# A two-layer token tower on one core: weight sums, head scales, spare products and low parts moved in the first attention

## The reference

```python
def act_quant(x):                       # one scale for the last axis
    scale = 127.0 / clip(max(abs(x), -1), 1e-5)
    return clip(round(x * scale), -128, 127) / scale
def bit_linear(x, W):                   # weights become -s, 0, +s
    s = clip(mean(abs(W)), 1e-5)
    return x @ (clip(round(W / s), -1, 1) * s).T
xq = act_quant(x)                       # x: the normalised tokens, 16 heads of 32
q, k, v = (act_quant(heads(bit_linear(xq, W))) for W in (Wq, Wk, Wv))
w = act_quant(softmax(q @ k.T / sqrt(32)))
y = act_quant(w @ v)                    # 4 positions of a sample attend to each other
x = x + act_quant(bit_linear(y, Wp))
# then: scores = x @ router_w, two of 16 experts; silu(x @ gate) * (x @ up) @ down
```

## Time and profile before

| | us |
| --- | --- |
| median of 3 runs | 303.21 |
| lowest, highest | 302.82, 305.16 |
| the profiled execution | 305.13 |
| its span, first to last instruction | 303.3 |
| TensorE, VectorE, ScalarE, GpSimd busy | 277.0, 237.1, 145.0, 14.4 |
| mean granted TensorE clock | 0.977 |

### The profile page before, as it was taken

One profiled execution on the slowest core, in us unless ns is written; L12 is line 12 of the kernel. 1 busy time (PEld: TensorE's weight loads), 2 busy tenths in 40 slices (PEclk: granted clock), 3 DMA queues, 4 the chain that ended last, 5 costly groups with the idle time before them and its releaser, 6 DMA issues. The chain is left out here.

```text
span 303.3 us, 4708 instructions
## 1 busy us (share of the span) xinstructions
PE 277.0 (91%) x1814; PEld 239.3 (79%) x1814; DVE 237.1 (78%) x438; ACT 145.0 (48%) x236; POOL 14.4 (5%) x32
## 2 busy tenths in 40 slices
PE   8988279959989999999999999987899999999993
PEld 3743144959988899999999988866799999999862
DVE  1789998593876999899989896698627896787683
ACT  2879550102844556556555423332128783673640
POOL 0200230010000000000000002300000000000000
PEclk9999789977999999999999999999999999999999
DMA  7940499912208466354520019276000000000003
GB/s 248 414 180 1 99 399 418 421 82 105 105 1 314 130 225 265 109 210 133 196 89 1 2 45 424 86 264 290 2 0 2 0 3 0 2 0 3 0 0 69
DMA packets 6567, 40.47 MB, mean 133 GB/s; under 512 B 1169, under 2 KB 1425, under 8 KB 5266
## 3 DMA queue, kind: packets, MB, share of 16 engines
q1 hardware_dynamic: 6546, 40.18, 35.1%
HBM read 39.13 MB, written 0.52 MB: 131 GB/s over the span
## 5 line engine op out<-in xcount | busy, mean ns | idle before, releaser
L870 PE MATMUL bank<-s_xt_hi,s_gu_hi 128*128 128x256 f32 x120 | 34.0, 283 | 0.0
L871 PE MATMUL bank<-s_xt_lo,s_gu_hi 128*128 128x256 f32 x120 | 33.9, 283 | 0.0
L872 PE MATMUL bank<-s_xt_hi,s_gu_lo 128*128 128x256 f32 x120 | 33.9, 282 | 0.0
L984 PE MATMUL bank<-s_xf_hi,s_f_hi 128*128 128x256 f32 x128 | 31.3, 283 | 0.1
L984 PE MATMUL bank<-s_xf_hi,s_f_lo 128*128 128x256 f32 x128 | 31.1, 281 | 0.0
L465 ACT CAST s_xt_hi<-bank 128x512 fp32r<-128x512 f32 x10 | 5.9, 587 | 42.4 <-PE bank L672 36.6
L984 PEld LDWEIGHTS bank<-s_xf_hi,s_f_hi 128*128 128x128 f32 x128 | 24.1, 188 | 0.7 <-ACT s_xf_hi L623 0.3
L984 PEld LDWEIGHTS bank<-s_xf_hi,s_f_lo 128*128 128x128 f32 x128 | 24.1, 188 | 0.3
L1480 DVE TENSOR_TENSOR s_f_lo<-s_ffn_raw,s_f_hi 128x1024 fp32r<-128x1024 f32 x16 | 19.6, 1225 | 6.1 <-ACT s_f_hi L596 6.1
L871 PEld LDWEIGHTS bank<-s_xt_lo,s_gu_hi 128*128 128x128 f32 x120 | 23.0, 191 | 0.2
L870 PEld LDWEIGHTS bank<-s_xt_hi,s_gu_hi 128*128 128x128 f32 x120 | 23.0, 191 | 0.3
(11 more groups left out here) (251 smaller groups left out, 731.0 us busy)
## 6 DMA issues: line engine op xcount, KB each, us to landing
s_moe_raw<-moe_gu SPq DMA_DIRECT2D x16, 768.0 KB, 5.9
s_ffn_raw<-ffn_w SPq DMA_DIRECT2D x4, 2048.0 KB, 9.9
s_moe_raw<-moe_dn SPq DMA_DIRECT2D x8, 768.0 KB, 4.4
s_big_raw<-att_w SPq DMA_DIRECT2D x4, 1024.0 KB, 8.3
s_big_raw<-down_w SPq DMA_DIRECT2D x1, 4096.0 KB, 25.1
s_l_raw<-l_w SPq DMA_DIRECT2D x1, 2560.0 KB, 15.1
out<-s_h SPq DMA_DIRECT2D x4, 128.0 KB, 2.3
s_tok_w<-tok_w SPq DMA_DIRECT2D x1, 256.0 KB, 2.7
```

What stands on the lines that cost most here:

```text
L870: pe.matmul(dst, w_hi, xt_hi[:, k, :], start=(k == 0), stop=False)
L871: pe.matmul(dst, w_hi, xt_lo[:, k, :], start=False, stop=False)
L872: last = pe.matmul(dst, w_lo, xt_hi[:, k, :], start=False, stop=(k == KC - 1))
L984: pe.matmul(tb(j, n)[:, 0:TOK], M[w][j][:, k, n * P:(n + 1) * P], M["xf_hi"][:, k, :], start=(w == "w_hi" and k == 0), stop=False)
```

## The change

Sums: weight 2's magnitudes are summed on ScalarE, all four there and in order; weight 3's sum stands ahead of the high parts of experts 0 and 1. Scales: `head_scales` is split into `floors` (a floor for each token, from the weight scale), `head_factors` (what rounding needs) and `head_steps` (g3). VectorE's order changes: weight scale 1 behind both tokens' rounding, weight scale 2 behind Q's rounding, the first key products ahead of V. ScalarE takes the exponential ahead of the four copies of weight 3. Low parts of experts 0 and 1 go from GpSimd to VectorE, behind xt_low(3); unit 0 starts on the high weights alone. Spare products: other counts.

```diff
 GpSimd
-            pool.wait_ge(k16_ready, TILES)
-            for e in range(2):
-                pool.wait_ge(guh_ready, e + 1)
-                if e == 1:
-                    pool.wait_ge(qk_done, 3)
-                pool.tensor_tensor(B["gu_lo"][e][:], main_of(e), B["gu_hi"][e][:].bitcast(F32), ALU.subtract
-                                   ).then_inc(gu_ready, 1)
 ScalarE
             abs_sum(0)
             abs_sum(1)
-            for m in range(2):
-                for n in range(2):
-                    side(m, n)
+            for n in range(2):
+                side(0, n)
+            abs_sum(2)
+            for n in range(2):
+                side(1, n)
             act.wait_ge(qx_ready, 2)
             for n in range(2):
                 side(2, n)
+            abs_sum(3)
             main_high(0)
             main_high(1)
-            abs_sum(3)
...
             for n in range(2):
                 side(3, n)
+            exp(0, A["sc"][:, 2], A["sc"][:, 3])
             for k in range(KC):
                 act.wait_ge(tern_done, k + 1)
                 act.copy(A["tern_p"][:, k, :], tern_bank(k)[:]).then_inc(tern_ready, 1)
-            exp(0, A["sc"][:, 2], A["sc"][:, 3])
 TensorE
-            early_warm(26)
+            early_warm(10)
             weight_total(0, bank[3][:, 0:1])
-            early_warm(16)
+            early_warm(12)
...
             project(0, 0, 0)
-            early_warm(8)
+            early_warm(4)
             project(0, 1, 0)
...
             weight_total(2, bank[3][:, 0:1])
+            early_warm(6, bank[1])
             for n in range(2):
                 for t in range(TILES):
                     project(1, n, t)
+                early_warm(6, bank[1])
             pe.wait_ge(half_ready, 3)
             for n in range(2):
                 for t in range(TILES):
                     project(2, n, t)
+                early_warm(6, bank[1])
             weight_total(3, bank[5][:, 0:1])
-            early_warm(8, bank[1])
+            early_warm(12, bank[1])
...
                 if t == 0:
-                    keep_warm(bank[3], GAP)
+                    keep_warm(bank[3], 3)
...
-                if part < 2:
+                if n == 0:
+                    pe.wait_ge(guh_ready, 1)
+                elif part < 2:
...
+                    first_products(0, xt_hi, True, False)
                     pe.wait_ge(xt_ready, 4)
                     router_low(1).then_inc(router_done, 1)
...
+                    first_products(0, xt_lo, False, False)
+                    pe.wait_ge(gu_ready, 1)
+                    first_products(1, xt_hi, False, True)
 VectorE
+            def floors(m):
+                o.settle()
+                o.mark(dve.tensor_scalar(c3[:, m, :], am[:, 3, :], A["sw"][:, m:m + 1], 63.5 / Q_EPS, ALU.mult, ALU.mult))
+                o.settle()
+                o.mark(dve.reciprocal(re3[:, m, :], c3[:, m, :]))
+            def head_factors(m):
+                o.settle()
+                o.mark(dve.scalar_tensor_tensor(am3[:, m], am3[:, m], 1.0 / 127.0, by_token(re3, m), ALU.mult, ALU.max))
+                o.settle()
+                o.mark(dve.reciprocal(f3[:, m], am3[:, m]))
+                o.settle()
+            def head_steps(m):
+                o.settle()
+                dve.scalar_tensor_tensor(g3[:, m], am3[:, m], Q_EPS / 127.0, by_token(c3, m), ALU.mult, ALU.mult
+                                         ).then_inc(g_ready, 1)
...
             token_scale(1)
             token_round(1)
+            weight_scale(1, bank[7][:, 0:1])
...
             transposed_out(1)
-            dve.wait_ge(ld_att[2], 16)
-            dve.tensor_reduce(A["asum"][:, 2:3], big_raw[:, 2 * KC * C:3 * KC * C], AX, ALU.add, apply_absolute_value=True
-                              ).then_inc(abs2_done, 1)
             largest(0, 0)
+            floors(0)
+            largest(0, 1)
+            head_factors(0)
+            head_round(0, q16_ready)
             weight_scale(2, bank[3][:, 0:1])
-            largest(0, 1)
-            head_scales(0)
-            head_round(0, q16_ready)
+            head_steps(0)
+            floors(1)
+            floors(2)
+            dve.wait_ge(g_ready, 1)
+            o.mark(dve.tensor_scalar(sh[:, 5], g3[:, 0], float(D) ** -0.5, None, ALU.mult))
             largest(1, 0)
             largest(1, 1)
-            head_scales(1)
+            head_factors(1)
             head_round(1, k16_ready)
+            head_steps(1)
             dve.wait_ge(q16_ready, TILES)
             dve.wait_ge(k16_ready, TILES)
             key_products(0, k16)
+            largest(2, 0)
+            largest(2, 1)
+            head_factors(2)
+            head_round(2, v16_ready)
+            head_steps(2)
+            weight_scale(3, bank[5][:, 0:1])
...
+            main_low(0)
+            main_low(1)
             rest_low(0)
```

More of the change, by code:

```diff
@@ L210, in tower @@
                 A["c3"] = sb("c3", [P, 3, TILES], F32, s2)
+                A["re3"] = sb("re3", [P, 3, TILES], F32, s2)
                 A["qkv"] = [sb(f"{n}16", [P, TILES, C], I16, s2) for n in "qkv"]
@@ L726, in weight_total @@
             def weight_total(m, dst):
[L727 to L730, removed]
+                pe.wait_ge(abs_done, m + 1)
                 pe.matmul(dst, onesf[:], A["asum"][:, m:m + 1], start=True, stop=True).then_inc(tot_done, 1)
@@ L850, in unit, with first_products @@
                 if n == 0:
[L851 to L856, removed]
+                    def first_products(i, x, first, last):
+                        for up, done in ((0, gate_done), (1, up_done)):
+                            for k in range(KC):
+                                ins = pe.matmul((up_bank if up else gate_bank)(n)[:, 0:TOK],
+                                                tuple(half_weights(n, k, up))[i], x[:, k, :],
+                                                start=(first and k == 0), stop=(last and k == KC - 1))
+                            if last:
+                                ins.then_inc(done, 1)
+                    first_products(0, xt_hi, True, False)
                     pe.wait_ge(xt_ready, 4)
                     router_low(1).then_inc(router_done, 1)
[L859 to L864, removed]
+                    first_products(0, xt_lo, False, False)
+                    pe.wait_ge(gu_ready, 1)
+                    first_products(1, xt_hi, False, True)
                     return
@@ L1129, in largest, with by_token @@
                                          apply_absolute_value=True))
-            def head_scales(m):
+            def floors(m):
                 o.settle()
-                o.mark(dve.tensor_scalar(c3[:, m, :], am[:, 3, :], A["sw"][:, m:m + 1], 0.5, ALU.mult, ALU.mult))
+                o.mark(dve.tensor_scalar(c3[:, m, :], am[:, 3, :], A["sw"][:, m:m + 1], 63.5 / Q_EPS, ALU.mult, ALU.mult))
                 o.settle()
-                c3b = c3[:, m, :].unsqueeze(2).to_broadcast([P, TILES, H])
-                o.mark(dve.tensor_tensor(am3[:, m], am3[:, m], c3b, ALU.mult))
+                o.mark(dve.reciprocal(re3[:, m, :], c3[:, m, :]))
+            def by_token(ap, m):
+                return ap[:, m, :].unsqueeze(2).to_broadcast([P, TILES, H])
+            def head_factors(m):
                 o.settle()
-                o.mark(dve.tensor_scalar(g3[:, m], am3[:, m], Q_EPS, 1.0 / 127.0, ALU.max, ALU.mult))
+                o.mark(dve.scalar_tensor_tensor(am3[:, m], am3[:, m], 1.0 / 127.0, by_token(re3, m), ALU.mult, ALU.max))
                 o.settle()
-                dve.sem_inc(g_ready, 1)
-                o.mark(dve.reciprocal(f3[:, m], g3[:, m]))
+                o.mark(dve.reciprocal(f3[:, m], am3[:, m]))
                 o.settle()
-                o.mark(dve.tensor_tensor(f3[:, m], f3[:, m], c3b, ALU.mult))
+            def head_steps(m):
                 o.settle()
+                dve.scalar_tensor_tensor(g3[:, m], am3[:, m], Q_EPS / 127.0, by_token(c3, m), ALU.mult, ALU.mult
+                                         ).then_inc(g_ready, 1)
             def head_round(m, done):
@@ L1159, in _ @@
             transposed_out(1)
[L1160 to L1162 removed]
             largest(0, 0)
+            floors(0)
+            largest(0, 1)
+            head_factors(0)
+            head_round(0, q16_ready)
             weight_scale(2, bank[3][:, 0:1])
[L1165 to L1167 removed]
+            head_steps(0)
[3 more added lines that the diff above has]
+            o.mark(dve.tensor_scalar(sh[:, 5], g3[:, 0], float(D) ** -0.5, None, ALU.mult))
             largest(1, 0)
             largest(1, 1)
[L1170 removed]
+            head_factors(1)
             head_round(1, k16_ready)
+            head_steps(1)
+            dve.wait_ge(q16_ready, TILES)
+            dve.wait_ge(k16_ready, TILES)
+            key_products(0, k16)
             largest(2, 0)
             largest(2, 1)
+            head_factors(2)
+            head_round(2, v16_ready)
+            head_steps(2)
```

(7 more changed lines are left out.)

8 lines of the change are left out of this document (2 added, 6 removed).

## The result

| | us |
| --- | --- |
| median after, 9 executions | 300.95 (300.04 to 302.47) |
| median before, 9 executions of the same rounds | 305.10 (302.82 to 306.74) |
| ratio, 95% interval | 0.9895 (0.9864 to 0.9925) |
| forecast | 298.9, 296.8 to 301.6 |
| profiled execution and its span | 300.32, 298.5 (before 305.13, 303.3) |

The kernel is faster, by about 1.05% (the two medians alone would give 0.9864, the low end of the interval). The forecast said 1.42% (4.3 of 303.21), which is outside the interval, and 0.9895 of 305.10 is 301.9, above the range. Yet the two profiled executions differ by 4.8 us, more than the 4.3 forecast. The work behind the forecast is therefore tested link by link first, and then the question is why executions of one kernel differ by 2 us.

The account below looks back on a forecast made before the run. Before 75 us the first attention's chain (VectorE, ScalarE, TensorE between) sets the time, then TensorE. Gains of 2.5 (softmax and values) and 1.8 (fewer spare products), 4.3 us, off the 303.21 median gave 298.9, range 296.8 to 301.6.

Parts of the forecast that it names:

- Links up to Q: First attention up to Q's rounding: scale at about 10.8, 2.28 us reduction gone, rounding at 20.8, 3.5 us earlier.
- Projections: TensorE's K and V projections as the limit: V's projection 0.7 us later, K's rounding ending 27.2, V's 32.0.
- Softmax: Softmax and values' sum: argument at 38.75, sum starting at 42.85 behind 18 spare products, gain 2.5 us.
- GAP: Spare products before tile 1's transposes, cut from 20 to 3: transposes start earlier, gain 1.8 us.
- GpSimd: VectorE's two-element scale, slowed beside GpSimd's low part: 0.8 us on the path goes, included in the sum.
- Low parts on VectorE, loads: Experts' low parts moved to VectorE, later expert loads: off the path, cost 0, bounds -0.9 to +1.2.
- A: Rival, chance 0.12: 18 spare products before the values' sum run at low clock, 3.8 us; total 300.3.
- B: Rival, chance 0.17: low clock falls on the router's products before unit 0, 2.0 us lost; total 300.9.
- D: Rival, chance 0.03: fewer spare products let the clock drop, values' sum at half rate, +7.1 us; total 306.0.
- C: Rival, chance 0.08: no low clock in unit 0, 1.2 to 1.4 us won; total 297.6.

Follow-up runs that it names:

- after_no_spare6: Changed kernel without the five groups of 6 spare products between the projections: 301.19 us, ratio 0.9913 to the kernel before.
- before_again: The kernel before, nothing edited, run again for a second profiled execution: median 304.69 us, ratio 1.001.
- after_third: The changed kernel run once more, nothing edited: median 300.73 us, ratio 0.9912 to the kernel before.
- before_gap3: Kernel before with 3 spare products instead of 20 between the two tiles' output products: 301.43 us, ratio 0.9909.
- combined: Changed kernel plus 36 spare products awaiting weight 3's signs, 24 awaiting normalisation, 32 behind first transposes, router products spread, one spare between projections: 298.83 us, ratio 0.9828.
- fill_and_spread: Changed kernel plus 36 spare products awaiting weight 3's signs, 24 awaiting normalisation, 32 behind first transposes, router products spread between unit 0's: 300.09 us, ratio 0.9852.
- after_gap20: Changed kernel with 20 spare products instead of 3 put back between the two tiles' output products: 301.86 us, ratio 0.9927.
- after_sum2_dve: Changed kernel with weight 2's sum back on VectorE ahead of Q's largest: 302.01 us, ratio 0.9955 to the kernel before.

## Why the prediction was wrong

The links hold, one by one; what failed is the step from one execution to the median:

- *Links up to Q*: scale at 10.66 (10.8), Q's rounding at 20.71 (20.8), and the missing reduction worth 1.15 us rather than 2.28. Right.
- *Projections*: K's rounding ends at 26.90 (27.2), V's at 31.66 (32.0); V's projection ends 0.2 us later than before, not 0.7. Right in kind; the spare groups do cost 0.7, as after_no_spare6 shows.
- *Softmax*: argument at 38.17 (38.75), sum at 42.17 (42.85), held by the 18 spare products, as said. Gain 3.15, not 2.5; 0.3 of the difference may be weight 0, whose sum could start at 7.05 instead of 7.34.
- *GAP*: 1.79 to 1.80 us locally, as said (1.8).
- *GpSimd*: direction right, size not: 0.8 was its price in the old order; left in the new order it would be 2.0.
- *Low parts on VectorE, loads*: nothing, as said (no wait of TensorE for them in units 0 to 2); routing starts at 69.64, 6.25 us earlier.
- Together (3.15 and 1.80), unit 1 starts 4.99 us earlier and the profiled execution is 300.32 where "it becomes 300.8".

What failed is the last step, "The runs' median is what is asked: 303.21 - 4.3 = 298.9", with the sentence before the sum, "From there everything moves as it is". The chain was built on an execution of 305.13, in which unit 0 is at the low clock, and taken off a median from executions of a faster kind: before_again at 303.49 runs unit 0 at the full clock, 1.35 us shorter, and starts unit 1 1.66 us earlier. That low stretch is not a fixed part of the kernel. In half the executions of the kernel before the time is near 303.1; in all three profiles of the changed one unit 0 is low. So from before_again to after unit 1 starts 3.33 us earlier, the 4.99 less 1.66, and the execution is 3.17 us shorter, which is what the ratio says (1.05% of 303 is 3.2). The medians of the two faster groups, 303.10 and 300.49, give 2.6; what makes the last 0.6 is not known. The base was a second fault of the same step: 303.21 was a median of 3, two of them of the faster kind, while all 119 executions have 304.02 and the 9 of the result, six of them of the slower kind, 305.10. That these nine give a difference of medians of 4.15, close to 4.3, is luck of that mix.

Of the rivals, A happened in part of the executions (18 spare products in 3.81 us in after_third, as A had it, but 0.9 us more than in the profile of after, where they took 2.89 and not 2.39). B and D did not occur in the three profiles: the router's window is at 0.97 in the profile of after and the sum takes 7.03 us in all three. C was on the wrong side: I let the changed kernel win the 1.4 us of unit 0, while it is the kernel before that has them in its faster half, as the profile of before_again shows, one profile for that half. The Trainium skill (TensorE: Matmul & The Clock Gate, Part 1), by which the monitor runs free of the kernel's start, stood in the text as a remark and should have been weighed: the unedited kernels do spread over 2 us, with the low stretches at other places in each. Open stays why the changed kernel meets the low clock in unit 0 so regularly; three profiles and the missing executions below 300 say that it does, not why. Open too is why before_gap3's median gains 2.8 us by one 1.8 us link: its six executions lie within 0.9 us, so the upper levels are gone, and against an execution of the kernel before that also has unit 0 at the full clock its one profile gains 1.9.

## What to carry to other kernels

Subtract a link's gain from an execution of the kind it was read in: before taking it off a median, look where the low-clock stretches lie in the profile, and ask whether the median's executions have them too. Gains of 0.7 us on links vanished in the medians of six executions that lie 1.7 to 2.2 us apart, so read such a gain as a distance within the profile. Only combined shows them in its median; fill_and_spread, with TensorE's waits filled and thin products spread in the same way, does not, and why is open. Here a GpSimd subtraction held a VectorE operation with two SBUF inputs until it ended (2.14 us in one order, 1.02 in another), so its price was what was left of it at that moment, and the reordering of VectorE changed it.

## What was not expected of the hardware

- A 128x32 VectorE operation took 2.14 us instead of 0.19 beside one GpSimd subtraction, and the reductions from PSUM beside it took their usual 0.69.
- Products with 16 columns count as busy in the profile (3.40 of 3.40 us in 64.4 to 67.8), and yet the clock is at 0.53 in the stretch behind them; behind the same products in before_again and after_gap20 it is at 1.00.
- Weight 0 let ScalarE start at 7.05 to 7.80 us in 18 of the 20 profiles, but at 9.00 in after_no_spare6 and 9.89 in after_sum2_dve, and no edit changes its transfer; Q's rounding starts later by as much, up to 2.8 us.
- The same 26 spare products at the start took 4.05 us in one execution of the kernel before and 3.00 in the profile of before_gap3, whose edit comes only at 55 us.
